# Order of the conditional output tiles: from one tile at a time to pairs of tiles, in an adaptive-FFN kernel on one core

## The reference, cut to what matters

```
xc    = einsum('bsi,boi->bso', x, w_cond[ids])
probs = softmax(xc @ W_router.T);  combine = top-2 of probs, renormalised
h     = einsum('nd,erd->ner', xc, A) * combine[..., None]
out   = x + xc @ W_base.T + b_base + einsum('ner,eor->no', h, B) * 2.0
```

## Time and profile before

| what | us |
|---|---|
| median of 3 runs | 396.82 |
| the profiled execution | 396.74 |
| its span, first to last instruction | 394.9 |
| TensorE (PE) busy | 389.9 (99%) |
| weight loads (PEld) busy, beside PE | 332.1 (84%) |
| VectorE (DVE) busy | 305.3 (77%) |
| ScalarE (ACT) busy | 183.7 (47%) |
| granted TensorE clock, mean of the span | 1.000 |

### The profile page before, as it was taken

How to read it: one execution, slowest core, us unless ns; L and a number is a source line. 1 busy time by engine, 2 the same in 40 slices (tenths; PEclk the granted TensorE clock), 3 DMA queues, 4 the chain that set the end, 5 groups by cost and what they waited for, 6 DMA issues and landing times.

```text
span 394.9 us, 5677 instructions
## 1 busy us (share of the span) xinstructions
PE 389.9 (99%) x2174; PEld 332.1 (84%) x2174; DVE 305.3 (77%) x441; ACT 183.7 (47%) x282; POOL 40.1 (10%) x68
## 2 busy tenths in 40 slices
PE   8999999999999999999999999999999999999996
PEld 7888888888888888888888888888888888888885
DVE  4797967779699999984457786878867999999311
ACT  5777734748632434332146676356656224441000
POOL 0101100110000130021172000000000001301110
PEclk9999999999999999999999999999999999999999
DMA  7998782768430135586669877356073102462222
GB/s 259 391 341 310 282 299 80 272 217 309 146 106 0 54 115 173 192 289 218 218 222 369 337 240 240 108 168 244 15 266 122 41 1 80 162 185 80 82 80 80
DMA packets 21083, 72.96 MB, mean 185 GB/s; under 512 B 2816, under 2 KB 2832, under 8 KB 21056
## 3 DMA queue, kind: packets, MB, share of 16 engines
q1 hardware_dynamic: 15840, 55.58, 40.6%
q0 software_dynamic: 4928, 15.97, 11.3%
q10 hardware_dynamic: 288, 1.05, 0.7%
HBM read 64.20 MB, written 8.39 MB: 184 GB/s over the span
## 4 chain that ended last, share of the span: by engine, by line
PE 97%; DMA 1%; SPq 1%; DVE 0%; ACT 0%; issue 0%
PE bank_x L801 30%; PE bank_x L805 15%; PE bank_y L786 9%; PE bank_y L787 9%; PE bank_y L788 9%; PE bank_x L787 8%; PE bank_x L788 8%; PE bank_x L786 8%; PE bank_y L845 2%; DMA raw<-w_cond 1%; SPq L362 1%; PE bank_y L865 0%; DVE out_sb L587 0%; ACT wc_hl L490 0%; SPq L346 0%
## 5 line engine op out<-in xcount | busy, mean ns | idle before, releaser
L801 PE MATMUL bank_x<-x_hl,wc_hl 128*128 128x512 f32 x512 | 128.7, 392 | 0.6 <-ACT wc_hl L490 0.6
L536 DVE TENSOR_TENSOR wc_hl<-raw,wc_hl 128x1024 fp32r<-128x1024 f32 x90 | 108.4, 1221 | 19.0 <-ACT wc_hl L472 18.9
L472 ACT CAST wc_hl<-raw 128x1024 fp32r<-128x1024 f32 x90 | 93.4, 1050 | 55.6 <-DVE raw L540 23.1
L801 PEld LDWEIGHTS bank_x<-x_hl,wc_hl 128*128 128x128 f32 x512 | 92.2, 189 | 17.8 <-ACT wc_hl L490 1.2
L805 PEld LDWEIGHTS bank_x<-x_hl,wc_hl 128*128 128x128 f32 x512 | 70.0, 190 | 5.1
L805 PE MATMUL bank_x<-x_hl,wc_hl 128*128 128x256 f32 x512 | 71.5, 282 | 0.0
L424 POOL DMA_DIRECT2D out<-out_sb x28 | 15.3, 545 | 249.8 <-DVE out_sb L587 228.5
L504 ACT COPY xc_low<-bank_x 128x256 f32<-128x256 f32 x64 | 23.6, 369 | 32.6 <-PE bank_x L805 32.6
L786 PE MATMUL bank_x<-x_hl,wc_hl 128*128 128x512 f32 x96 | 37.3, 389 | 0.0
L787 PE MATMUL bank_x<-x_hl,wc_hl 128*128 128x512 f32 x96 | 37.3, 389 | 0.0
L788 PE MATMUL bank_x<-x_hl,wc_hl 128*128 128x512 f32 x96 | 37.3, 389 | 0.0
(11 more groups left out here) (91 smaller groups left out, 481.6 us busy)
## 6 DMA issues: line engine op xcount, KB each, us to landing
raw<-w_cond SPq DMA_DIRECT2D x62, 512.0 KB, 4.6
raw<-w_base SPq DMA_DIRECT2D x24, 512.0 KB, 5.2
out_sb<-x POOLq DMA_DIRECT2D x32, 256.0 KB, 5.1
raw<-x SPq DMA_DIRECT2D x14, 512.0 KB, 4.6
out<-out_sb POOLq DMA_DIRECT2D x28, 256.0 KB, 2.3
raw<-x ACTq DMA_DIRECT2D x2, 512.0 KB, 3.6
raw<-w_cond SPq DMA_DIRECT2D x4, 256.0 KB, 3.6
out<-out_sb SPq DMA_DIRECT2D x4, 256.0 KB, 2.0
```

The source lines that it names most:

```text
L472: nc.scalar.copy(split_dst(key, HI), split_src(key)).then_inc(hi_done, 1)
L536: nc.vector.tensor_tensor(split_dst(key, LO), split_src(key), split_dst(key, HI).bitcast(F32), ALU.subtract).then_inc(lo_done, 1)
L801: nc.tensor.matmul(ps[:], wc_hl[:, slot_of(s, t), HI, k], x_hl[:, s % 2, k].rearrange("p h n -> p (h n)"), start=(k == 0), stop=False)
```

## The change

The tiles of a sequence are now taken in lists from `COND_TILES`. An even sequence has four pairs, (0,1), (2,3), (4,5), (6,7); an odd one has the pairs (0,1), (2,3) and then the single tiles 4, 5, 6, 7. TensorE runs, for a pair, the 8 wide matmuls of the first tile, the 8 wide ones of the second, the 8 narrow ones of the first and the 8 narrow ones of the second. ScalarE and VectorE work by pairs too: the first tile's copy or sum, the first tile's splits, the second tile's copy or sum, then the casts or low parts of both tiles, and then the second tile's splits. For the pair (6,7) the splits of both tiles stand at the end. `gate_h` and `h_high` come after the pair (2,3), `h_low` after the pair (4,5), the spreading of the gate after the pair (0,1). The split "bd" moves from step (2,6) to step (2,7), behind w(3,3). The number of instructions and their operands stay as they are. In the diff below the part with `act` is ScalarE's, the one with `dve` VectorE's, and `cond` TensorE's.

```
+COND_TILES = [[(0, 1), (2, 3), (4, 5), (6, 7)], [(0, 1), (2, 3), (4,), (5,), (6,), (7,)]]
...
-    if (s, t) == (2, 6):
+    if (s, t) == (2, 7):
         items = items + [("bd", 0, 0)]
...
+def early_splits(s, tiles):
+    return step_splits(s, tiles[0]) if tiles[0] < KT - 2 else []
+
+def late_splits(s, tiles):
+    steps = [t for t in tiles[1:] if t < KT - 2]
+    if tiles[-1] == KT - 1:
+        steps += [KT - 2, KT - 1]
+    return [key for t in steps for key in step_splits(s, t)]
...
+                        for t in tiles:
+                            act.wait_ge(cond_done, s * KT + t + 1)
+                            nc.scalar.copy(xc_low[:, t % 2], bank_x[t % HT][:, TOK:]).then_inc(low_copied, 1)
+                            if t == tiles[0]:
+                                for key in early_splits(s, tiles):
+                                    hi(key)
+                        for t in tiles:
+                            act.wait_ge(xc_summed, s * KT + t + 1)
+                            nc.scalar.copy(xc_hl[:, t, HI, s % 2 * TOK:(s % 2 + 1) * TOK],
+                                           xp[:, s // 2 % 2, t, s % 2 * TOK:(s % 2 + 1) * TOK]).then_inc(xc_hi, 1)
+                        for key in late_splits(s, tiles):
                             hi(key)
...
+                        for t in tiles:
+                            dve.wait_ge(low_copied, s * KT + t + 1)
...
+                            if t == tiles[0]:
+                                split(early_splits(s, tiles))
+                        for t in tiles:
+                            dve.wait_ge(xc_hi, s * KT + t + 1)
...
+                        split(late_splits(s, tiles))
...
+            def cond(s, tiles):
+                for t in tiles:
+                    pe.wait_ge(hi_done, SPLIT["w", s, t])
+                    if t == 0:
+                        pe.wait_ge(lo_done, SPLIT["x", s, 0])
+                        pe.wait_ge(lo_done, SPLIT["x", s, 1])
+                    ps = cond_bank(s, t)
+                    for k in range(KT):
+                        wide(ps, s, t, k)
+                for t in tiles:
+                    pe.wait_ge(lo_done, SPLIT["w", s, t])
+                    for k in range(KT):
+                        mm = narrow(bank_x[t % HT], s, t, k)
+                    mm.then_inc(cond_done, 1)
```

More of the change, by code:

```diff
@@ L497, in _ @@
                 for s in range(GSEQS * g, GSEQS * (g + 1)):
-                    for t in range(KT):
-                        c = s * KT + t + 1
-                        if (s, t) == (0, 6):
+                    for tiles in COND_TILES[s % 2]:
+                        if s == 0 and KT - 2 in tiles:
                             act.wait_ge(consts_in, 16)
                             nc.scalar.copy(expand[:], const_sb[:, C_EXP:C_EXP + P]).then_inc(expand_in, 1)
[L503 to L511, removed]
+                        for t in tiles:
[9 more added lines that the diff above has]
+                        for key in late_splits(s, tiles):
                             hi(key)
-                        if s % GSEQS == 2 and t == 2:
+                        if s % GSEQS == 2 and tiles[0] == 2:
                             h_high(2 * g)
@@ L682, in _ @@
                 for s in range(GSEQS * g, GSEQS * (g + 1)):
[L683 to L696, removed]
+                    for tiles in COND_TILES[s % 2]:
+                        for t in tiles:
+                            dve.wait_ge(low_copied, s * KT + t + 1)
+                            nc.vector.tensor_tensor(xp[:, s // 2 % 2, t, s % 2 * TOK:(s % 2 + 1) * TOK],
+                                                    bank_x[t % HT][:, 0:TOK], xc_low[:, t % 2], ALU.add) \
+                                .then_inc(xc_summed, 1)
+                            if t == tiles[0]:
+                                split(early_splits(s, tiles))
+                        for t in tiles:
+                            dve.wait_ge(xc_hi, s * KT + t + 1)
+                            xc_of = xc_hl[:, t, :, s % 2 * TOK:(s % 2 + 1) * TOK]
+                            nc.vector.tensor_tensor(xc_of[:, LO], xp[:, s // 2 % 2, t, s % 2 * TOK:(s % 2 + 1) * TOK],
+                                                    xc_of[:, HI].bitcast(F32), ALU.subtract).then_inc(xc_lo, 1)
+                        split(late_splits(s, tiles))
+                        if s % GSEQS == 2 and tiles[0] == 2:
                             gate_h(2 * g)
-                        if s % GSEQS == 2 and t == 3:
+                        if s % GSEQS == 2 and tiles[0] == 4:
                             h_low(2 * g)
@@ L916, in _ @@
                 for s in range(GSEQS * g, GSEQS * (g + 1)):
[L917 to L923, removed]
+                    for tiles in COND_TILES[s % 2]:
+                        if s == 0 and tiles[0] == 0:
+                            first_cond()
+                        else:
+                            cond(s, tiles)
+                        if s % GSEQS == 2 and tiles[0] == 0:
                             gate_to_rows(2 * g)
```

## The result

The changed kernel takes 397.52 us (median of 22 runs), the kernel before 396.70 (22 runs): 0.82 us more, ratio 1.002 with a 95% interval of 1.0015 to 1.0026. It is slower, a little less than forecast (+0.99).

A forecast was written before the change was run, and what follows sets the result against it. The prediction took TensorE as the bound, busy 389.9 of 394.9 us and never waiting in the conditional stage. Its terms, -0.46 + 1.10 + 0.35 = +0.99, gave 397.8 us, range 396.5 to 398.3.

The forecast's parts named there:

- TensorE's spacing: Conditional stage: each of 23 pairs saves one narrow-to-wide change, taken as 0.02 us, together 0.46 us less.
- rival (c): TensorE's pairs: no gain in spacing, sixteen narrow matmuls costing as much as twice eight; 398.27 us, chance 0.13.
- The wait at (3,(2,3)): Start of pair (2,3) in s=3: ScalarE casts w(3,2) too late, so TensorE's weight load starts 1.1 us late.
- The second router: Router after s=3: VectorE's sum of tile 7 comes late for its last step, 0.35 us, bounds 0 to 0.7.
- No wait elsewhere: Rest of the conditional stage: other casts and sums have cover, no TensorE wait above 0.1 us.
- Rival (a): s=2: VectorE's idle time covers the work, both waits go, only the -0.46 stays; 396.36 us, chance 0.20.

The follow-up runs named there:

- all_pairs: The h_late kernel with all eight tiles of the odd sequences in pairs too, 31 pairs instead of 23: 396.13 us, kernel before 396.89.
- b_late: The changed kernel with the split of low-rank matrix b at step (2,6), behind w(3,2), instead of (2,5): 397.55 us, kernel before 396.84.
- h_late: The changed kernel with ScalarE's h_high issued after the pair (4,5) instead of (2,3), in s=2 and 6: 396.26 us, kernel before 396.80.
- interleave1: The kernel before, single tiles, with wide and narrow matmuls in strict turn inside each tile: 399.39 us, kernel before 396.80.

## Why the prediction was right

The time, its sign and both mechanisms came as forecast. By its steps:

1. *TensorE's spacing, -0.46.* Right: 23 pairs at 0.020 are 0.46. The size owes something to luck: the step saved is 0.026, and the 0.007 that the narrow blocks give back, which the prediction did not have, brings it to the 0.02 that it took from rounded rows. A longer narrow block adds nothing to the recovery, so rival (c) fell; all_pairs adds eight pairs and eight times the 0.02. The Trainium skill ("TensorE: Matmul & The Clock Gate", section "Back-to-back issue gap") leaves no price for the order of the same matmuls; three orders of one tile took 2.793, 2.813 and 2.83 here, so the measurement decides against it. The prediction read the section too simply, though: it gives the 109 ns for a matmul by itself, and says that in a stream with weight loads this counts too little for small matmuls and too much for 512 columns. The 119 ns here for 256 columns lies on the side that it names; the 227 ns for 512, over its 216, does not.
2. *The wait at (3,(2,3)), 1.10.* Right in place, cause and size: 0.93 of gap and 0.10 in the first spacing behind it, with about 0.02 of slower matmuls after that, 1.06.
3. *The second router, 0.35.* Right in place and cause, mis-sized by 0.12: it cost 0.23. The weight load was 0.34 late, nearly as walked, but the sum counted that as time lost and left out the 0.11 by which such a load runs ahead of its matmul. That the lateness itself fits is partly luck: on the forecast's clock the sum of tile 7 was done at 107.39 (107.54 walked) and the load was wanted at 107.10 (107.24), each about 0.15 early. b_late shows this wait to be the other face of the first: remove one and the other grows.
4. *No wait elsewhere.* Right, w(7,2) with its 0.1 of cover too: the pair (7,(2,3)) starts without a gap. Behind the start-up TensorE waits for no load of SyncE's.
5. *Rival (a), that VectorE's idle time would cover it.* It failed in the changed kernel, but its idle time was there to be used: h_late moves one ScalarE step and comes out as case (a) has it, 396.26 for its 396.36. The prediction saw that ScalarE reached the copy of tile 4 at 78.19 with the tile done at 75.7, and did not ask what that gap was worth.

The sum by the trace: -0.46 + 1.06 + 0.23 = +0.83, the measured difference being 0.82.

## What to carry to other kernels

When the bound engine never waits, its helpers' lists can be walked from start-to-start distances: here twenty steps of s=2 came within 0.05 us; a longer walk drifts, as the end of s=3 did by 0.15. Batching work on the bound engine hands its helpers their work in lumps, so look for the stretch where the helper that nearly keeps up has extra steps, and for a cross-engine wait with ready work queued behind it: moving that one step was worth 1.36 us, where the change had lost 0.82. A wait removed by reordering comes back later if the helper's chain is as long as before; shorten the chain instead.

## What the runs showed of the hardware

In the interleave1 trace the same sixteen matmuls in strict turn run at two speeds. Up to tile (3,3) a tile takes 2.82 to 2.83, then a low part comes 0.05 late and the next tiles, up to the router, take 2.77; the tiles of s=4 to 7 take 2.81 to 2.83 again. TensorE's starts in tile (3,2), then in tile (3,4):

```profile
90.08 0.40 PE L801 MATMUL bank_x<-x_hl,wc_hl 128*128 128x512 f32 x1
90.32 0.28 PE L805 MATMUL bank_x<-x_hl,wc_hl 128*128 128x256 f32 x1
...
91.14 0.40 PE L801 MATMUL bank_x<-x_hl,wc_hl 128*128 128x512 f32 x1
...
97.81 0.39 PE L801 MATMUL bank_x<-x_hl,wc_hl 128*128 128x512 f32 x1
98.04 0.28 PE L805 MATMUL bank_x<-x_hl,wc_hl 128*128 128x256 f32 x1
...
98.85 0.39 PE L801 MATMUL bank_x<-x_hl,wc_hl 128*128 128x512 f32 x1
```

Three couples of wide and narrow take 1.06 (90.08 to 91.14), later 1.04 (97.81 to 98.85), with a granted clock of 1.00 in both. In the changed kernel, the wide matmuls after the wait at (3,2) need nine spacings after the first long one to come back to 0.227, where five do after a narrow block. What sets this recovery was not tried; that it depends on what went before, and not on the instructions alone, is all that these traces show.
